# One signal per head instead of one per pair behind the first exponential of a gated cross-attention block

## The reference

```
x = x + tanh(g_xattn) * xattn(layernorm(x), ctx)
x = x + tanh(g_ffn)   * ffn(layernorm(x))
# inside xattn, per head (112 queries, 375 keys)
qk = Q @ K.T
scores  = qk / 4
feats   = [mean(scores), mean(max(scores)), mean(var(softmax(scores), ddof=1))]
t       = exp(clip(mlp(feats)))            # one temperature for each head
attn    = softmax(qk / (2 * t)) @ V        # then the output projection
# ffn: silu(q(h) @ q(Wg)) * (q(h) @ q(Wu)), quantised again, @ q(Wd)
```

## Time and profile before

| what | us |
|---|---|
| median of 3 runs | 810.11 |
| lowest and highest of them | 806.78, 812.03 |
| span of the profiled execution | 806.5 |
| busy PE / DVE / ACT / POOL in that span | 708.8 / 720.1 / 691.7 / 520.3 |
| first scores of the first pass, last of them (start) | 24.4, 642.9 |

### The profile page before, as it was taken

One profiled execution on the slowest core, in us unless ns is written; L12 is line 12 of the kernel. 1 busy time (PEld: TensorE's weight loads), 2 busy tenths in 40 slices (PEclk: granted clock), 3 DMA queues, 4 the chain that ended last, 5 costly groups with the idle time before them and its releaser, 6 DMA issues.

```text
span 806.5 us, 20948 instructions
## 1 busy us (share of the span) xinstructions
PE 708.8 (88%) x7117; PEld 475.3 (59%) x7127; DVE 720.1 (89%) x1479; ACT 691.7 (86%) x1482; POOL 520.3 (65%) x983
## 2 busy tenths in 40 slices
PE   7568889999999999999999999999998888777886
PEld 5234566666666666666666666666665555433444
DVE  5789899979899898989999999899999868798996
ACT  1578789898999999999999999999898997678884
POOL 4757556667777667676666676767663145376985
PEclk8666699999999999999999999999999999899999
DMA  9997847464667565767545666646563123156567
GB/s 206 202 259 179 176 123 148 106 114 129 153 119 145 123 141 123 147 115 151 127 129 141 126 130 133 128 128 138 114 124 73 45 72 97 52 124 165 137 164 176
DMA packets 148889, 108.50 MB, mean 135 GB/s; under 512 B 56992, under 2 KB 145184, under 8 KB 148768
## 3 DMA queue, kind: packets, MB, share of 16 engines
q1 hardware_dynamic: 143630, 101.98, 57.0%
q10 hardware_dynamic: 5152, 5.19, 2.6%
HBM read 49.54 MB, written 12.85 MB: 77 GB/s over the span
## 4 chain that ended last, share of the span: by engine, by line
PE 45%; DVE 22%; ACT 21%; issue 7%; DMA 2%; POOL 2%; SPq 1%; DVEq 0%; ACTq 0%; POOLq 0%
PE p_o L1327 9%; PE p_m L1405 9%; ACT ex L1179 7%; PE p_s L1310 7%; ACT pt L1169 6%; PE p_t L1348 5%; DVE kst L1015 4%; DVE hmax L1018 4%; PE p_m L1394 4%; DVE stats L890 3%; PE p_m L1386 3%; ACT L1169 2%; ACT L1206 2%; PE p_m L1378 2%; DVE nm L909 2%
## 5 line engine op out<-in xcount | busy, mean ns | idle before, releaser
L1179 ACT ACTIVATE ex<-p_s,nm 112x375 f32<-112x375 f32 x512 | 272.6, 606 | 10.1 <-DVE nm L909 8.9
L1169 ACT ACTIVATE pt<-p_t,ct 128x336 f32<-128x336 f32 x488 | 242.5, 563 | 32.4 <-PE p_t L1348 31.9
L890 DVE BATCH_NORM_STATS2 stats<-ex 112x6 f32<-112x375 f32 x512 | 253.2, 537 | 8.1 <-ACT ex L1179 6.6
L909 DVE TENSOR_REDUCE nm<-p_s 112x2 f32<-112x750 f32 x256 | 236.6, 925 | 2.0 <-PE p_s L1310 2.0
L1310 PE MATMUL p_s<-kst,qst 96*112 96x375 bf16 x512 | 135.8, 350 | 34.3 <-ACT ex L1179 24.8
L1348 PE MATMUL p_t<-qst,kst 99*128 99x112 bf16 x1464 | 115.3, 214 | 3.5 <-ACT pt L1169 2.7
L1348 PEld LDWEIGHTS p_t<-qst,kst 99*128 99x128 bf16 x1464 | 91.3, 98 | 42.9 <-issue 18.7
L1386 PE MATMUL p_m<-wv_sb,ctxt 128*128 128x256 f32 (+1 forms) x384 | 106.3, 400 | 4.0 <-DVE va L842 2.6
L1327 PE MATMUL p_o<-pt,va 128*32 128x112 f32 (+1 forms) x3072 | 102.0, 266 | 1.0 <-ACT ex L1179 0.5
L1405 PE MATMUL p_m<-ctxt,wk_sb 128*128 128x375 f32 x240 | 94.3, 517 | 1.3 <-DVE qf L858 0.7
L1327 PEld LDWEIGHTS p_o<-pt,va 128*32 128x32 f32 (+1 forms) x3072 | 70.8, 111 | 36.9 <-issue 30.7
(11 more groups left out here) (190 smaller groups left out, 1201.3 us busy)
## 6 DMA issues: line engine op xcount, KB each, us to landing
kst<-kp SPq DMA_DIRECT2D x378, 93.8 KB, 3.5
ctxt<-ctxt_dram SPq DMA_DIRECT2D x32, 375.0 KB, 4.2
qbounce<-qp SPq DMA_DIRECT2D x32, 168.0 KB, 2.7
qst<-qbounce SPq DMA_DIRECT2D x32, 168.0 KB, 3.6
qst<-qbounce SPq DMA_DIRECT2D x32, 112.0 KB, 3.4
xm<-x_dram SPq DMA_DIRECT2D x32, 112.0 KB, 2.4
x_dram<-x SPq DMA_DIRECT2D x32, 112.0 KB, 1.9
xt<-x_dram SPq DMA_DIRECT2D x28, 128.0 KB, 2.9
```

The lines of the kernel that those rows point to most:

```text
L890: last = nc.vector.bn_stats(stats[:, nb % RING, 2 * pb + i], ex[0:SQ, 2 * (t % 2) + i, :])
L909: nc.vector.tensor_reduce(nm[:, n % RING, 2 * p:2 * p + 2], p_s[t % 2][0:SQ, :, 0:SK], axis=AX.X, op=ALU.max, negate=True).then_inc(s_max, 1)
L1169: nc.scalar.activation(pt[:, (2 * r + i) % 8], st_home(r, i)[:, 0:KC * SQ].rearrange("k (c q) -> k c q", c=KC), ACT.Exp, scale=ct[:, nr % ...
L1179: last = nc.scalar.activation(ex[0:SQ, 2 * ((t - 1) % 2) + i, :], p_s[(t - 1) % 2][0:SQ, i, 0:SK], ACT.Exp, bias=nm[:, ne % RING, h:h + 1])
```

## The change

ACT increments `s_e1` after each of the 512 exponentials instead of after every second one. PE waits for head 0 of `t - 2`, writes what belongs to bank 0 (a riding transposition's chunk 0, if there is one, and the scores of head 0), then waits for head 1 and does the same for bank 1. With a riding transposition the order of four operations so changes from chunk 0, chunk 1, scores 0, scores 1 to chunk 0, scores 0, chunk 1, scores 1; the waits for the transposition's input stay ahead of all of them. The score signal `s_s` and the transposition signals still come once, from the second. DVE waits for `s_e1` ahead of each head's row statistics. The other waits on `s_e1` are counted anew for the same points. No arithmetic, tile or DMA changes.

```
+        def exps_done(t, i):
+            return 2 * t + i + 1
 # DVE
-                    dve.wait_ge(s_e1, count(SLOTS, nb, pb + 1))
                     for i in range(2):
+                        dve.wait_ge(s_e1, exps_done(t - 2, i))
                         last = nc.vector.bn_stats(stats[:, nb % RING, 2 * pb + i], ex[0:SQ, 2 * (t % 2) + i, :])
 # ACT
-                        last = nc.scalar.activation(ex[...], p_s[(t - 1) % 2][0:SQ, i, 0:SK], ACT.Exp, bias=nm[:, ne % RING, h:h + 1])
-                    last.then_inc(s_e1, 1)
+                        nc.scalar.activation(ex[...], ..., ACT.Exp, bias=nm[:, ne % RING, h:h + 1]).then_inc(s_e1, 1)
 # PE
-                if t >= 2:
-                    pe.wait_ge(s_e1, min(t - 1, SLOTS * B))
+                if t >= SLOTS * B:
+                    pe.wait_ge(s_e1, exps_done(min(t - 2, SLOTS * B - 1), 1))
...
+                for i in range(2):
+                    last = i == 1
+                    if 2 <= t < SLOTS * B:
+                        pe.wait_ge(s_e1, exps_done(t - 2, i))
+                    if back:
+                        turn = nc.tensor.transpose(ride_of(t, m5)[:, i, :], ong[:, i * P:(i + 1) * P], ident[0:SQ, 0:SQ])
+                        if last:
+                            turn.then_inc(s_ott, 1)
+                    if x is not None:
+                        turn = nc.tensor.transpose(ride[t % 2][:, i, :], xn[:, i * P:(i + 1) * P], ident[0:SQ, 0:SQ])
+                        if last:
+                            turn.then_inc(s_xt, 1)
+                    if 0 <= t < SLOTS * B:
                         h = 2 * p + i
-                        last = mm(p_s[t % 2][0:SQ, i, 0:SK], ...)
-                    last.then_inc(s_s, 1)
+                        scores = mm(p_s[t % 2][0:SQ, i, 0:SK], ...)
+                        if last:
+                            scores.then_inc(s_s, 1)
```

More of the change, by code:

```diff
@@ L1178, in slot @@
                         h = 2 * pe_ + i
-                        last = nc.scalar.activation(ex[0:SQ, 2 * ((t - 1) % 2) + i, :], p_s[(t - 1) % 2][0:SQ, i, 0:SK], ACT.Exp,
-                                                    bias=nm[:, ne % RING, h:h + 1])
-                    last.then_inc(s_e1, 1)
+                        nc.scalar.activation(ex[0:SQ, 2 * ((t - 1) % 2) + i, :], p_s[(t - 1) % 2][0:SQ, i, 0:SK], ACT.Exp,
+                                             bias=nm[:, ne % RING, h:h + 1]).then_inc(s_e1, 1)
                 if copying and 0 < t < BACK:
@@ L1280, in slot @@
                 mm = nc.tensor.matmul
-                if t >= 2:
-                    pe.wait_ge(s_e1, min(t - 1, SLOTS * B))
-                if p == OT_AT and 0 <= m5 < B:
+                if t >= SLOTS * B:
+                    pe.wait_ge(s_e1, exps_done(min(t - 2, SLOTS * B - 1), 1))
+                back, x = p == OT_AT and 0 <= m5 < B, turned(t)
+                if back:
                     pe.wait_ge(s_ong, count(1, m5, 1))
@@ L1288, in slot @@
                         pe.wait_ge(s_gc, TAILED)
[L1289 to L1292, removed]
                 if x is not None:
@@ L1298, in slot @@
                     pe.wait_ge(s_xn, count(1, x, 1))
[L1299 to L1308, removed]
-                        h = 2 * p + i
-                        last = mm(p_s[t % 2][0:SQ, i, 0:SK], qst[n % KRING][0:STACK, h, :], kst[n % KRING][0:STACK, h, 0:SK], start=True, stop=True)
-                    last.then_inc(s_s, 1)
+                if 0 <= t < SLOTS * B and p == 0:
+                    pe.wait_ge(s_kst[n % KRING], ring_count(192, n, KRING))
+                    pe.wait_ge(s_qst[n % KRING], ring_count(48, n, KRING))
+                for i in range(2):
+                    last = i == 1
+                    if 2 <= t < SLOTS * B:
+                        pe.wait_ge(s_e1, exps_done(t - 2, i))
+                    if back:
+                        turn = nc.tensor.transpose(ride_of(t, m5)[:, i, :], ong[:, i * P:(i + 1) * P], ident[0:SQ, 0:SQ])
[6 more added lines that the diff above has]
+                    if 0 <= t < SLOTS * B:
+                        h = 2 * p + i
+                        scores = mm(p_s[t % 2][0:SQ, i, 0:SK], qst[n % KRING][0:STACK, h, :], kst[n % KRING][0:STACK, h, 0:SK], start=True, stop=True)
+                        if last:
+                            scores.then_inc(s_s, 1)
+                if x is not None and t in FIRST_KEYS:
+                    first_key(*FIRST_KEYS[t])
                 r = t - BACK
@@ L1343, in scores_t @@
                         if t == TAIL + 1:
-                            pe.wait_ge(s_e1, SLOTS * B)
+                            pe.wait_ge(s_e1, 2 * SLOTS * B)
                         elif r > 0:
```

## The result

| | before | changed | ratio, 95% interval |
|---|---|---|---|
| first measurement, us | 808.44 (806.65 to 812.03, 4 runs) | 798.14 (796.11 to 799.68, 4 runs) | 0.9855, 0.9831 to 0.9878 |
| measured again, us | 810.14 (23 runs) | 801.11 (799.76 to 801.81, 6 runs) | 0.9885, 0.9863 to 0.9908 |

By these ratios the change makes the kernel 1.1 to 1.5% faster; the medians lie 10.3 and 9.0 us apart. The profiled execution of the changed kernel took 797.28 us with a span of 795.5.

The account below looks back on a forecast made before the run. No engine alone bounds it: the chain hops between PE, DVE and ACT. 0.16 + 0.15 + 0.10 us a period over twelve periods (4.9), plus 0.5 before and 0.8 behind, gave 6.2 us off 810.1: 803.9, range 800.5 to 810.

Parts of the forecast that it names:

- The bound: Whole kernel: no engine alone limits it; the chain hops between PE, DVE and ACT.
- The second place: Scores at 417.17, released by the exponential pair of 416.19: PE stands 0.15 us before it, so another 0.15 a period.
- the decisive slot of the first: Scores at 408.37, PE's last meeting with its signal there: this floor falls by 0.16 us, not more.
- DVE's wait as cover without gain: DVE's row statistics: the first start 0.3 us earlier, but later work waits for PE, so no time is gained.
- Satisfied waits and signals at nothing: The 254 PE waits, 256 DVE waits and 256 ACT increments cost nothing where already satisfied.
- the slower rival: Head 1's wait stops its weight load from starting under head 0's matmul: 0.05 us in 256 slots, 816.7; chance 0.06.
- What lies beyond the last exponential: After 643 us there are no first exponentials; no gain was counted there.
- until 414.3 ACT is rigid: ACT from 392.34 to 414.3 in a period: nothing PE does earlier brings one of its exponentials forward.
- my first place: Scores at 408.37, over `rl` at 410.23 to ACT's `pt` at 415.22: 0.16 us a period.
- the third place: Scores at 426.49, ahead of ACT's `pt` at 429.07: PE stands 0.10 us, so up to 0.10 a period.
- what lies outside the steady part: Chain hand-overs outside the twelve periods: three from 93.35 on, 0.5 us, and five behind 591, 0.8 us.
- The rival "more": Each place where PE stands for ACT counts, 57 and 12 waits at 0.16 us: 11.0 us, 799.1; chance 0.12.

Follow-up runs that it names:

- all waits and no early start: The changed kernel, but each per-head wait on PE and DVE asks for the second head's exponential: ratio 1.001, period 38.72 us.
- without pairs 1 and 2: PE waits per head in all slots but pairs 1 and 2 of odd batches, DVE for both heads: period 38.28 us, against 38.03 with none left out.
- PE's change alone: The changed kernel, but DVE's statistics wait for both heads and only PE waits per head: ratio 0.9887, period 38.03 us.
- DVE alone: The changed kernel, but PE waits for both heads and only DVE's statistics wait per head: ratio 1.0002, period 38.72 us.
- five slots: PE waits per head only in pairs 1, 2, 5 of odd and 1, 5 of even batches, DVE for both heads: period 38.16 us.
- without pair 5 of even batches: PE waits per head in all slots but pair 5 of even batches, DVE for both heads: period 38.22 us, against 38.03 with none left out.
- eleven-slot kernel: PE waits per head in all slots of a period but pairs 1, 2, 5 of odd and 1, 5 of even batches: period 38.72 us.

## Why the prediction was right and wrong

**Right.** The bound, and that a period is the unit. The mechanism: head 0's scores ahead of head 1's exponential, worth one matmul's 0.16 us at each hand-over however long the wait is; the steps measured 0.14 to 0.17 (at the slot with the rider PE gained more, 0.25, and ACT could use 0.17 of it). The second place (0.15 forecast, 0.16 lost when left out) and the decisive slot of the first (0.16, and 0.14). DVE's wait as cover without gain (ratio 1.0002). Satisfied waits and signals at nothing: the slower rival, in which head 1's wait stops its weight load, would have shown as 1% or more in the kernel with all waits and no early start, which measured 1.001. What lies beyond the last exponential: no change (160.07, 160.30 and 160.03 us). The page "TensorE: Matmul & The Clock Gate" of the Trainium skill has in its table at the top the window in which PE pulls weight loads ahead of matmuls. The trace agrees, and a wait already met doesn't hinder it: in the changed kernel the weight load of head 0's scores, with its wait for `ex` met, starts at 409.29, and the `p_t` matmuls ahead of it run from 409.04 to 409.50.

**Wrong: the step "until 414.3 ACT is rigid".** It was read from a timeline without idle brackets. ACT had two waits in it, for the keys and for `p_t`, of 0.16 to 0.18 us each. One of them, at `kf`, is a step of its own that I did not have, and it makes the sum of a period 0.64 instead of 0.41 together with the next point. The experiments that leave slots out show it: without pairs 1 and 2 the period loses 0.25 us at that instruction alone, 0.18 of it the step. The other wait is the one at the `pt` of 412.38. There the gain of my first place arrives, not by the path that I had given it, over DVE's `rl` to the `pt` of 415.22.

**Mis-sized: the third place.** I had 0.10, the time for which PE stood before 426.49. It measured 0.14 to 0.15, and 0.19 when left out. I had let the scores' weight load begin one step of 0.05 behind the last `p_t` matmul. It begins with it. In the changed kernel the group at 409.04 starts its last matmul at 409.29 (five steps of 0.05), and so does the weight load of head 0's scores:

```profile
409.29 0.13 PEld L1317 LDWEIGHTS p_s<-kst,qst 96*112 96x112 bf16 x1
```

Before, the group of 426.10 would have let it begin at 426.35, and it began at 426.49. So it had stood some 0.15, as before 417.17.

**Mis-sized: what lies outside the steady part.** I had 1.3 us for it and 4.9 for twelve periods. With 0.64 in twelve periods and the same 1.3 the sum would have been 9.0 us and the time 801.1, inside my range and where the second measurement lies (801.11). That they agree so closely is in part luck, because the start-up scatters by more. The ten periods from slot 64 on measured 6.4 us and the last 31 slots 1.2; slots 24 to 64 gave 2.7 to 3.6. Not all of that can be shown to be the change's work: the start-up scatters by 1.8 us between two profiles of the same kernel, and the fall of the clock near 165 us came in the kernel before and in five of the experiments (all waits and no early start, DVE alone, five slots, and the two without pairs 1 and 2 and without pair 5 of even batches), three of which have most of the gain. The eleven-slot kernel, whose period is no shorter than 38.72, had no such fall and took 58.05 us from slot 40 to 64; DVE alone, with the same period and the fall, took 58.88, and the kernel before 58.89. So a fall costs some 0.8 us there, and the changed kernel's profiles were without it. Whether the change makes the fall rarer stays open: both profiles of the changed kernel and that of PE's change alone were without it, but so were five others, two of them without any gain in the period. The first measurement lies 3 us below the 801.1; its profile has 2.0 us more between slots 24 and 64 than the periods there give, and the fall is some 0.8 of them. The rest of the 3 us stays open.

**The rival "more"**, with 0.12, named the right direction and gave 799.1, but not the mechanism: it counted every place where PE stands for ACT, and the eleven-slot kernel shows that most of these give nothing. The count that holds is of places where ACT in turn waits for what PE does next.

## What to carry to other kernels

Look for hidden waits by start-to-start distances: if an instruction that follows the same predecessor usually starts 0.92 us after it and here starts 1.09, it waits, though no idle time is shown. Splitting a pair's wait is worth the later half's work on the waiting engine and not the wait's length, and only where an engine in turn waits for what follows; where a slot is split and the next one is not, the second can give back what the first won. Before a small loss is put down to one of several things that were changed together, look for a kernel that has the loss without it: here the kernel with riders in the old order showed the loss that I had put down to the new one. When a kernel repeats a pattern, the length of one period in a single profile tells apart variants by 0.02 us, where the time of runs scatters by 5.

## What the runs showed of the hardware

ACT's exponentials of 112 by 375 last 0.6 us but start 0.46 apart, so that an engine that looks full can wait some 0.16 us behind a pair of them unseen (1.09 from the pair's start to the next instruction's, against 0.92). A fall of PE's granted clock to 1.2 GHz in the steady part cost 1.5 us in a period of 38.8. A weight load whose wait is already met is pulled ahead under running matmuls (at 409.29, under `p_t` matmuls that run to 409.50), and 254 more waits on PE, 256 on DVE and 256 signals on ACT gave a ratio of 1.001. Alternating float32 transpositions and bf16 score matmuls instead of running them two and two cost 0.01 us at most: 0.58 us from the first weight load to what follows, against 0.57. But that weight load started 0.07 us later after the reload (9.34 against 9.27) in both kernels whose wait for `ex` is whole, as it was, but stands behind the wait for the transposition's input; no run moves that wait alone.
